# Key lookup: every second tile's eight rows of values fetched by indirect DMA and summed on VectorE

## The chip, the cores and the metric

The kernel runs on one core of one Trainium2 chip. The time is that of the device from start to end, in microseconds, the median of three runs. The engines are TensorE (PE in the rows, its weight loads PEld), VectorE (DVE), ScalarE (ACT), GpSimd (POOL) and SyncE (SP), which issues the transfers. Lines such as L2246 are lines of the kernel before; the changed kernel has 47 lines more, so the same function stands some 30 to 50 lines lower in it.

## The reference

A two-layer model: a Mamba block, a mixture-of-experts attention, a rotary attention, and last a lookup of keys, the only part that the change touches. T is 4096 tokens of width 256. Cut to what matters:

```
x3     = x2 + context @ Wo.T + bo                  # end of the attention layer
xh     = layernorm(x3)
query  = xh @ q_proj.T                             # 128 wide
scores = (query @ R.T) @ (keys @ R.T).T / sqrt(48) + reliability   # 1024 keys
top, idx = top_k(scores, 8)
look   = sum_k softmax(top)_k * values[idx_k]      # values: 1024 rows of 256
learned = unc_w2 . gelu(xh @ unc_w1.T + b1)        # one number a token
gate   = sigmoid(f(sigmoid(learned), log(1 + var(xh)) / its mean))
out    = x3 + xh + gate * look
```

## The kernel before

The lookup is the function key_lookup, the last of the program. It takes the 4096 tokens in 8 chunks of 512 tokens, each of 4 tiles of 128 tokens (a token lies on a partition). Every engine has its own program, written out by hand in one fixed order, and the engines wait for each other by semaphores alone. Chunks 0 to 5 run in loops on the hardware; chunks 6 and 7 are written out.

Per chunk: flip_ctx and x3_pair (twice, two tiles each) make x3 in the PSUM bank pX, and add puts it into SBUF on VectorE. normalize is the layernorm: four statistics, seven small operations, one power on GpSimd (L2188), four normalizing operations (L92). flip_xh, move_xh, project, route and move_rq make the router's query of the chunk; widen, hidden and learn make the learned number. keep stores x3 + xh and its statistics.

Per tile: scores multiplies 128 tokens by 1024 keys into one of two PSUM buffers (pS). pick takes the eight largest on VectorE (MAX8, L2231) and writes a copy in which these eight are replaced by a mark (MATCH_REPLACE8, L2233). expo takes the exponential of all 1024 scores on ScalarE. weigh (L2239) multiplies it by "is marked", which leaves eight weights among 1024 zeros, and sums them. flip_weights turns the 128 x 1024 weights over on TensorE, move_weights copies them to SBUF, lookup multiplies them by all 1024 rows of values (L2510, 16 passes through the array), and finish (L2246) scales the result by one over the sum.

The body of VectorE's loop shows in which order this goes for one chunk:

```
weigh(n + 1, 1); pick(n + 2, 0, base); finish(n, 0)
weigh(n + 2, 0); pick(n + 3, 1, base + TILE_MARKS); finish(n + 1, 1)
keep(c + 1, base)
weigh(n + 3, 1); pick(n + 4, 0, base); add(c + 2, 0); finish(n + 2, 0)
add(c + 2, 1); normalize(c + 2, base)
weigh(n + 4, 0); pick(n + 5, 1, base); finish(n + 3, 1); learned(c + 1)
```

GpSimd does two things a chunk: the bias (L2186) on the loaded x2, and the power of the layernorm. At the end results (L2272) makes the output, four operations a chunk, once the gate is known.

Of the kernel before, what the change touches and what calls it, by code (L numbers as in the profile page):

```python
# [12 lines left out]
ALU = mybir.AluOpType  # L13
ACT = mybir.ActivationFunctionType
AXIS_X = mybir.AxisListType.X
ds = bass.ds
# [5 lines left out]
NT = T // TILE  # L22
# [2098 lines left out]
def key_lookup(nc, a, p):  # L2121
# [3 lines left out]
    GONE = -3.0e38  # L2125
    with Scope(nc, "look") as s:
# [8 lines left out]
        top, ntop = s.sb("top", [128, 2, TOP]), s.sb("ntop", [128, 2])  # L2135
        left, expd, weight = s.sb("left", [128, 2, NK]), s.sb("expd", [128, 2, NK]), s.sb("weight", [128, 2, NK])
# [21 lines left out]
        out_ready, winv_ready = s.sem("out_ready"), s.sem("winv_ready")  # L2158
        one_set = s.sem("one_set")
# [5 lines left out]
        with nc.Block() as block:  # L2165
# [13 lines left out]
            def _(pool):  # L2179
# [4 lines left out]
                with pool.Fori(0, NCH) as c:  # L2184
                    pool.wait_ge(c_in, (c + 1) * 32)
                    nc.gpsimd.tensor_tensor(x2[:], x2[:], b_o[:].unsqueeze(1).broadcast_to([128, TPC, D]), ALU.add).then_inc(biased, 1)  # L2186
                    pool.wait_ge(var_ready, c + 1)
                    nc.gpsimd.tensor_tensor(rstd[:], var[:], mhalf[:], ALU.pow).then_inc(rstd_ready, 1)  # L2188

            KEEP_MARKS = TPC + 2  # L2190
# [3 lines left out]
            def _(dve):  # L2194
# [30 lines left out]
                def pick(n, b, base):  # L2225

                    ch = Chain(dve, dve_sem, base)
                    at_least(dve, weight_ready, n - 1)
                    dve.wait_ge(s_psum, n + 1)
                    ch.mark(nc.vector.memset(wsum[:, b:b + 1], 0.0))  # L2230
                    ch.step(nc.vector.max(top[:, b, :], pS[:, b, :]))  # L2231
                    nc.vector.tensor_scalar(ntop[:, b:b + 1], top[:, b, 0:1], -1.0, None, ALU.mult).then_inc(ntop_ready, 1)
                    nc.vector.match_replace(out=left[:, b, :], in_to_replace=top[:, b, :], in_values=pS[:, b, :], imm_value=GONE).then_inc(left_ready, 1)  # L2233
                    assert ch.n == TILE_MARKS

                def weigh(n, b):
                    dve.wait_ge(exp_ready, n + 1)
                    at_least(dve, wt_psum, n - 1)
                    nc.vector.scalar_tensor_tensor(weight[:, b, :], left[:, b, :], GONE, expd[:, b, :], ALU.is_equal, ALU.mult, accum_out=wsum[:, b:b + 1]).then_inc(weight_ready, 1)  # L2239
                    dve.wait_ge(weight_ready, n + 1)  # L2240
                    nc.vector.reciprocal(winv[:, ds(n, 1)], wsum[:, b:b + 1]).then_inc(winv_ready, 1)

                def finish(n, b):
                    dve.wait_ge(winv_ready, n + 1)
                    dve.wait_ge(look_psum, n + 1)
                    nc.vector.tensor_scalar(look_all[:, ds(n, 1), :], pL[:, 0:D], winv[:, ds(n, 1)], None, ALU.mult).then_inc(look_ready, 1)  # L2246
# [433 lines left out]
```

## Time and profile before

| | |
|---|---|
| median of 3 runs | 3569.22 us (3567.5 to 3570.5) |
| the profiled execution | 3561.59 us, its span 3559.8 us |
| key lookup in the span | from 3213.8 us to 3555.35 us |
| busy in the whole span | TensorE 91%, VectorE 77%, ScalarE 63%, GpSimd 27% |

The profiled execution is one of many, 7.6 us below the median of the runs. Differences of about 0.2% (7 us) are what a measurement of this kernel can tell from none. The lookup is some 340 us of it; shares over the whole span say little about it.

### The profile page before, as it was taken

How to read it: one execution, taken by the hardware profiler on the slowest of the kernel's cores; microseconds unless marked ns; L12 is line 12 of the kernel's file. 1: busy time of each engine (PE TensorE's matmuls, PEld its weight loads, DVE VectorE, ACT ScalarE, POOL GpSimd, SP SyncE). 2: the span in 40 equal slices, each digit the busy share in tenths (PEclk: the TensorE clock that was granted, in tenths of full speed). 3: DMA queues.
4: the chain of work that ended last, by engine and by line, in shares of the span. 5: the costliest groups of instructions: out<-in, count | busy, mean ns of one | idle time of the engine just before them, and what ended most of it. 6: DMA issues, size and time to landing. Idle time of an engine off the chain costs nothing. (4 is left out here: it accounts for less than half of the span.)

```text
span 3559.8 us, 54793 instructions
## 1 busy us (share of the span) xinstructions
PE 3222.1 (91%) x17996; PEld 1622.3 (46%) x18162; DVE 2750.6 (77%) x4129; ACT 2234.5 (63%) x3972; POOL 965.3 (27%) x907
## 2 busy tenths in 40 slices
PE   7868888988899998998799999999999999997897
PEld 3327777777566666775322222222222222224665
DVE  6739999999466664456888888888888888854666
ACT  5669999999100002222278888888788888883343
POOL 7639999998000000003200000000000000001100
PEclk9979999999899999999889999999999999998999
DMA  4656443420311416422400000000000000001001
GB/s 136 197 176 149 119 109 96 105 62 13 113 57 35 104 32 155 118 60 75 124 8 14 21 14 22 15 21 15 22 15 21 15 21 14 26 4 33 29 24 48
DMA packets 219079, 216.75 MB, mean 61 GB/s; under 512 B 63986, under 2 KB 165490, under 8 KB 218036
## 3 DMA queue, kind: packets, MB, share of 16 engines
q1 hardware_dynamic: 218820, 213.41, 21.9%
q8 instruction: 149, 2.44, 0.3%
q14 instruction: 110, 0.90, 0.1%
HBM read 145.99 MB, written 67.37 MB: 60 GB/s over the span
## 5 line engine op out<-in xcount | busy, mean ns | idle before, releaser
L1975 DVE TENSOR_REDUCE attn_part_max<-attn_pM 128x1 f32<-128x1024 f32 x1024 | 1204.4, 1219 | 162.8 <-PE attn_pM L2029 159.3
L1955 ACT ACTIVATE attn_probs<-attn_pE 128x512 f32<-128x512 f32 x2048 | 1089.8, 597 | 205.7 <-PE attn_pE L2078 196.4
L2078 PE MATMUL attn_pE<-attn_q,attn_k_exp 128*128 128x512 bf16 x1882 | 590.5, 385 | 54.6 <-ACT attn_q L1927 24.7
L2049 PE MATMUL attn_pA<-attn_probs,attn_v 128*32 128x512 f32 x4096 | 560.7, 604 | 2.0 <-issue 1.0
L648 DVE TENSOR_TENSOR_SCAN scan_h<-scan_abar,scan_states,scan_dbu 128x512 f32<-128x512 f32 x384 | 458.3, 1252 | 0.0
L2078 PEld LDWEIGHTS attn_pE<-attn_q,attn_k_exp 128*128 128x128 bf16 x2048 | 139.1, 97 | 609.0 <-ACT attn_probs L1955 462.4
L662 PE MATMUL scan_hT<-scan_ident,scan_h 128*128 128x128 f32 x2048 | 322.5, 281 | 71.3 <-ACT scan_hcT L600 29.0
L1908 POOL TENSOR_TENSOR attn_peak_parts<-attn_peak,attn_zero 128x4 bf16<-128x4 f32 x128 | 26.4, 206 | 1278.2 <-DVE attn_peak L1979 1278.2
L600 ACT ACTIVATE scan_hcT<-scan_hT,scan_c_t 128x512 f32<-128x512 f32 x512 | 366.4, 716 | 1.1 <-PE scan_hT L662 1.1
L2028 PE MATMUL attn_pM<-attn_k_exp,attn_q 64*128 64x512 bf16 x1024 | 326.1, 392 | 23.3 <-DVE attn_part_max L1975 15.1
L1173 PE MATMUL moe_pP<-moe_w_qkv,moe_xT 128*128 128x384 f32 x1024 | 340.3, 490 | 0.9
L2029 PE MATMUL attn_pM<-attn_k_max,attn_q 64*128 64x512 bf16 x1024 | 326.1, 392 | 0.0
L672 PE MATMUL scan_y_acc<-scan_ident,scan_hcT 128*128 128x128 f32 x2048 | 304.2, 274 | 1.2 <-DVE scan_g_even L631 0.6
L662 PEld LDWEIGHTS scan_hT<-scan_ident,scan_h 128*128 128x128 f32 x2048 | 224.2, 142 | 167.9 <-DVE scan_h L648 112.4
L589 POOL TENSOR_TENSOR scan_dbu<-scan_du_odd,scan_b_odd 128x2048 f32<-128x2048 f32 x64 | 289.7, 4557 | 8.9 <-DVE scan_h L648 8.9
L589 POOL TENSOR_TENSOR scan_dbu<-scan_du_even,scan_b_even 128x2048 f32<-128x2048 f32 x64 | 289.2, 4553 | 7.3 <-DVE scan_h L648 5.2
L1173 PEld LDWEIGHTS moe_pP<-moe_w_qkv,moe_xT 128*128 128x128 f32 x1024 | 193.5, 191 | 131.7 <-DVE moe_acc L1043 4.3
L672 PEld LDWEIGHTS scan_y_acc<-scan_ident,scan_hcT 128*128 128x128 f32 x2048 | 240.6, 143 | 4.6 <-issue 2.5
L1046 DVE SCALAR_TENSOR_TENSOR moe_acc<-moe_pP,moe_rw,moe_acc 128x192 f32<-128x192 f32 x448 | 161.9, 411 | 76.2 <-PE moe_pP L1173 75.5
L2028 PEld LDWEIGHTS attn_pM<-attn_k_exp,attn_q 64*128 64x128 bf16 x1024 | 83.1, 93 | 293.8 <-issue 158.5
L613 ACT ACTIVATE scan_abar<-scan_delta_even,scan_decay 128x512 f32<-128x512 f32 x256 | 188.9, 738 | 7.9 <-DVE scan_h L648 7.9
L613 ACT ACTIVATE scan_abar<-scan_delta_odd,scan_decay 128x512 f32<-128x512 f32 x256 | 182.7, 714 | 8.5 <-DVE scan_h L648 8.5
(282 smaller groups left out, 3874.4 us busy)
## 6 DMA issues: line engine op xcount, KB each, us to landing
scan_b_even<-mid_BC SPq DMA_DIRECT2D x16, 1024.0 KB, 10.2
scan_b_odd<-mid_BC SPq DMA_DIRECT2D x16, 1024.0 KB, 9.6
causal_rwB<-mid_rwT SPq DMA_DIRECT2D x64, 256.0 KB, 4.5
attn_q<-mid_q_parts SPq DMA_DIRECT2D x224, 64.0 KB, 2.4
mid_gT<-front_gT SPq DMA_DIRECT2D x8, 1024.0 KB, 8.4
mid_uT<-front_uT SPq DMA_DIRECT2D x8, 1024.0 KB, 9.7
mid_dT<-scan_g_odd SPq DMA_DIRECT2D x8, 1024.0 KB, 4.3
moe_yT<-mid_yT SPq DMA_DIRECT2D x7, 1024.0 KB, 6.7
```

The lines of the kernel that those rows point to most:

```text
L589: nc.gpsimd.tensor_tensor(dbu[:, G % NDBU, :, :], du[u % 2][:], b_row, ALU.mult).then_inc(dbu_ready, 1)
L600: nc.scalar.activation(hcT[:, i % NHC, :], hT[:, i % 2, :], ACT.Copy, scale=c_t[:, u * TPC + tile, n:n + 1]).then_inc(hc_ready, 1)
L613: nc.scalar.activation(abar[:, k % 2, :], delta[u % 2][:, m, :], ACT.Exp, scale=decay[:, m, n:n + 1]).then_inc(abar_ready, 1)
L648: nc.vector.tensor_tensor_scan(h[:, G % NH, m, :], abar[:, k % 2, :], dbu[:, G % NDBU, m, :], state, ALU.mult, ALU.add).then_inc(scan_done, 1)
L662: last = nc.tensor.transpose(hT[:, i % 2, m * 128:(m + 1) * 128], h[:, G % NH, m, tile * 128:(tile + 1) * 128], ident[:])
L672: last = nc.tensor.matmul(y_acc[:, m, tile * 128:(tile + 1) * 128], hcT[:, i % NHC, m * 128:(m + 1) * 128], ident[:], start=(n == 0 and ti ...
L1173: last = nc.tensor.matmul(pP[:, n % NP, 0:2 * QKV], xT[:, c % 2, k, j * 128:(j + 1) * 128], w_qkv[:, k, pr * 2 * QKV:(pr + 1) * 2 * QKV], ...
L1955: nc.scalar.activation(probs[:, kt % 4, h, :], pE[:, bank(item), :], ACT.Exp, scale=SCALE).then_inc(exp_done, 1)
L1975: nc.vector.reduce_max(part_max[:, h, j, i:i + 1], pM[:, m % 2, :], AXIS_X).then_inc(max_read, 1)
L2028: nc.tensor.matmul(pM[:, m % 2, 0:CH], q[0:64, qc, h, j * 128:(j + 1) * 128], k_exp[0:64, par, i * CH:(i + 1) * CH], start=True, stop=True)
L2049: last = nc.tensor.matmul(pA[32 * h:32 * h + 32, :], v[:, par, kt, :], probs[:, kt % 4, h, :], start=(kt == 0), stop=(kt == KT - 1))
L2078: nc.tensor.matmul(pE[:, bank(item), :], k_exp[:, par, kt * 128:(kt + 1) * 128], q[:, qc, h, :], start=True, stop=True).then_inc(e_psum, 1)
```

## The change

Of the four tiles of a chunk, tiles 0 and 2 ("even") are done as before. Tiles 1 and 3 ("odd") are no longer weighed, flipped, moved and multiplied. Instead place_top takes the eight largest scores and their places (MAX_INDEX), expo_top takes the exponential of the eight alone, gather issues eight indirect DMAs from GpSimd (each fetches one row of values for each of the 128 tokens, 128 KB), and add_rows sums the eight rows by their weights on VectorE. add_rows of a tile stands one odd tile later in the order than its place_top. pS keeps two buffers: one for even tiles, one for odd ones. GpSimd's loop is written out. The core of the diff:

```diff
+                def gather(o):
+
+                    pool.wait_ge(place_ready, o + 1)
+                    pool.wait_ge(sum_ready, AHEAD + o - 1)
+                    for k in range(TOP):
+                        nc.gpsimd.indirect_dma_start(rows[:, o % 2, k, :], None, a["values"], bass.IndirectOffsetOnAxis(place[:, o % 2, k:k + 1], 0)).then_inc(rows_in[o % 2], 16)
+
+                for c in range(2):
+                    bias(c)
+                    root(c)
+                gather(0)
+                for c in range(NCH):
+                    if c + 2 < NCH:
+                        bias(c + 2)
+                    gather(2 * c + 1)
+                    if c + 2 < NCH:
+                        root(c + 2)
+                    if c + 1 < NCH:
+                        gather(2 * c + 2)
...
+                def place_top(c, j):
+
+                    o, b = 2 * c + j // 2, j // 2 % 2
+                    dve.wait_ge(s_psum, c * TPC + j + 1)
+                    nc.vector.memset(gate8[:], 0.0).then_inc(cleared, 1)
+                    nc.vector.max(top8[:, b, :], pS[:, 1, :]).then_inc(top8_ready, 1)
+                    dve.wait_ge(top8_ready, o + 1)
+                    nc.vector.tensor_scalar(ntop8[:, b:b + 1], top8[:, b, 0:1], -1.0, None, ALU.mult).then_inc(ntop8_ready, 1)
+                    nc.vector.max_index(place[:, b, :], top8[:, b, :], pS[:, 1, :]).then_inc(place_ready, 1)
...
+                def add_rows(c, j):
+
+                    o, b = 2 * c + j // 2, j // 2 % 2
+                    dst = look_all[:, ds(c * TPC + j, 1), :]
+                    dve.wait_ge(exp8_ready, o + 1)
+                    nc.vector.reciprocal(inv8[:, b:b + 1], sum8[:, b:b + 1]).then_inc(sum_step, 1)
+                    dve.wait_ge(sum_step, o * SUM_STEPS + 1)
+                    nc.vector.tensor_scalar(w8[:, b, :], e8[:, b, :], inv8[:, b:b + 1], None, ALU.mult).then_inc(sum_step, 1)
+                    dve.wait_ge(sum_step, o * SUM_STEPS + 2)
+                    dve.wait_ge(rows_in[b], (c + 1) * 16 * TOP)
+                    nc.vector.tensor_scalar(dst, rows[:, b, 0:1, :], w8[:, b, 0:1], None, ALU.mult).then_inc(sum_step, 1)
+                    for k in range(1, TOP):
+                        dve.wait_ge(sum_step, o * SUM_STEPS + 2 + k)
+                        nc.vector.scalar_tensor_tensor(dst, rows[:, b, k:k + 1, :], w8[:, b, k:k + 1], dst, ALU.mult, ALU.add).then_inc(sum_step if k < TOP - 1 else sum_ready, 1)
...
+                    pick(c, 2, base)
+                    finish(c, 0)
+                    weigh(c, 2)
+                    place_top(c, 3)
+                    base = base + TILE_MARKS
+                    keep(c + 1, base)
+                    base = base + KEEP_MARKS
+                    pick(c, 4, base)
+                    base = base + TILE_MARKS
+                    add_rows(c, 1)
                     if ahead == 2:
                         add(c + 2, 0)
-                    finish(n + 2, 0)
+                    finish(c, 2)
                     if ahead == 2:
                         add(c + 2, 1)
                         normalize(c + 2, base)
                         base = base + CHUNK_LN_MARKS
...
+                    weigh(c, 4)
+                    place_top(c, 5)
+                    add_rows(c, 3)
+                    learned(c + 1)
```

In the last chunk add_rows(7, 1) stands ahead of the first results and add_rows(7, 3) ahead of the last four.

The first place is TensorE, from the middle of the loop's chunk: before, the query's product (L2479, project) is followed by a tile's flip of weights (look_pT<-look_ident,look_weight), its scores (look_pS) and later its lookup (look_pL).

```order
L2448 MATMUL look_pT<-look_ident,look_xh 128x128 x8
L2510 MATMUL look_pL<-look_values,look_weightT 128x256 x8
L2479 MATMUL look_pX<-look_xT,look_w_q 128x512 x2
L2460 REGISTER_ALU
L2448 MATMUL look_pT<-look_ident,look_weight 128x128 x8
L2503 MATMUL look_pS<-look_rk,look_rq 128x512 x2
L2484 MATMUL look_pX<-look_query,look_w_r 128x512
L2452 ISA
L2448 MATMUL look_pT<-look_ident,look_ctx 128x128 x8
L2510 MATMUL look_pL<-look_values,look_weightT 128x256 x8
L2489 MATMUL look_pX<-look_xT,look_w_u 64x512 x2
```

The same place on TensorE after the change, where L2529 is project, L2558 scores and L2566 lookup.

```order
L2497 MATMUL look_pT<-look_ident,look_xh 128x128 x8
L2566 MATMUL look_pL<-look_values,look_weightT 128x256 x8
L2526 REGISTER_ALU
L101 REGISTER_ALU
L2529 MATMUL look_pX<-look_xT,look_w_q 128x512 x2
L2558 MATMUL look_pS<-look_rk,look_rq 128x512 x2
L2534 MATMUL look_pX<-look_query,look_w_r 128x512
L2501 ISA
L2497 MATMUL look_pT<-look_ident,look_ctx 128x128 x8
L2539 MATMUL look_pX<-look_xT,look_w_u 64x512 x2
```

The flip and the lookup of tile 1 are gone; the scores of tile 3 still stand behind project, which waits for the copy of xh.

The second place is VectorE, in the loop behind keep: before, a tile's weigh is followed by the next pick and the first add.

```order
L2239 SCALAR_TENSOR_TENSOR look_weight,look_wsum<-look_left,look_expd 128x1024
L2241 ISA
L2241 RECIPROCAL look_winv<-look_wsum 128x1
L2229 REGISTER_ALU
L2230 MEMSET look_wsum 128x1
L2231 MAX look_top<-look_pS 128x8
L44 REGISTER_ALU
L2232 TENSOR_SCALAR look_ntop<-look_top 128x1
L2233 MATCH_REPLACE look_left<-look_top,look_pS 128x1024
```

After the change VectorE has there the pick of an even tile and then add_rows; the last two rows come seven times in all.

```order
L2265 MAX look_top<-look_pS 128x8
L44 REGISTER_ALU
L2266 TENSOR_SCALAR look_ntop<-look_top 128x1
L2267 MATCH_REPLACE look_left<-look_top,look_pS 128x1024
L2299 RECIPROCAL look_inv<-look_sum 128x1
L2300 ISA
L2301 TENSOR_SCALAR look_w<-look_e,look_inv 128x8
L2302 REGISTER_ALU
L2303 ISA
L2304 ISA
L2304 TENSOR_SCALAR look_look_all<-look_rows,look_w 128x256
L2306 REGISTER_ALU
```

Ten operations in a row, each of which waits for the one before it, now stand between the pick and the first add.

The third place is GpSimd after the change: the start and two chunks (L2196 bias, L2200 the power of the layernorm, L2207 the gathers).

```order
L2196 TENSOR_TENSOR look_x<-look_x,look_b_o 128x1024
L2200 TENSOR_TENSOR look_rstd<-look_var,look_mhalf 128x4
L2207 DMA look_rows<-in_values,look_place 128x256 x8
L2196 TENSOR_TENSOR look_x<-look_x,look_b_o 128x1024
L2207 DMA look_rows<-in_values,look_place 128x256 x8
L2200 TENSOR_TENSOR look_rstd<-look_var,look_mhalf 128x4
```

The power, for which VectorE's layernorm waits, now stands behind sixteen gathers a chunk; before, only the bias stood ahead of it.

## Rows read from the trace of the kernel before

**Rows 1.** The chain that ended last, in order of time: start us, us, what

```profile
3331.28 1.03 POOL look_rstd L2188
...
3359.56 1.92 PE look_pX L2471 x8
...
3421.32 1.09 ACT look_xT L2358 x2
...
3422.63 1.98 PE look_pX L2479 x4
...
3484.14 1.03 POOL look_rstd L2188
```

**Rows 2.** Busy time by window: two chunks, then the last stretch; last columns clock, DMA share, GB/s

```profile
3367.62:3443.93 76.31, 68.40 (x326) 48.87 (x328) 50.65 (x125) 30.35 (x42) 7.66 (x4) 0.98 0.08 27
3484.14:3555.35 71.21, 58.03 (x265) 42.42 (x263) 51.50 (x122) 27.85 (x38) 1.02 (x1) 0.93 0.15 52
```

**Rows 3.** Waits of four chunks: engine line waited for, us in total, times, longest

```profile
DVE look_look_all L2246 <- PE look_pL L2510: 26.0, 12, 3.4
```

**Rows 4.** Groups by line, lookup stage: count, then busy us, mean ns, then idle

```profile
L2510 PE MATMUL look_pL<-look_values,look_weightT 128*128 128x256 f32 x512 | 126.2, 403 | 8.6 <-ACT look_weightT L2358 4.5 <-DVE look_look_all L2246 4.1
...
L2272 DVE SCALAR_TENSOR_TENSOR look_result<-look_look_all,look_gate,look_sum_all 128x256 f32<-128x256 f32 x32 | 12.9, 474 | 1.9 <-ACT look_gate L2440 1.8
```

**Rows 5.** Timeline of VectorE, one chunk: start us, us, engine, line, operation

```profile
3366.70 0.76 DVE L2200 TENSOR_TENSOR look_x<-look_pX,look_x 128x256 f32<-128x256 f32 x2 [1.05 <-PE look_pX L2471]
...
3370.93 1.38 DVE L92 TENSOR_SCALAR look_xh<-look_x,look_st,look_rstd 128x256 f32<-128x256 f32 x4 [1.13 <-POOL look_rstd L2188]
3372.53 1.22 DVE L2239 SCALAR_TENSOR_TENSOR look_weight<-look_left,look_expd 128x1024 f32<-128x1024 f32 x1 [0.23 <-DVE look_xh L92]
...
3373.91 0.16 DVE L2241 RECIPROCAL look_winv<-look_wsum 128x1 f32 x1
...
3374.05 1.23 DVE L2231 MAX8 look_top<-look_pS 128x8 f32<-128x1024 f32 x1
3375.32 0.15 DVE L2232 TENSOR_SCALAR look_ntop<-look_top 128x1 f32<-128x1 f32 x1
...
3376.59 0.47 DVE L2246 TENSOR_SCALAR look_look_all<-look_pL,look_winv 128x256 f32 x1
...
3377.91 1.22 DVE L2239 SCALAR_TENSOR_TENSOR look_weight<-look_left,look_expd 128x1024 f32<-128x1024 f32 x1 [0.77 <-ACT look_expd L2390]
...
3394.42 1.22 DVE L2214 TENSOR_TENSOR look_sum_all<-look_x,look_xh 128x1024 f32 x1
...
3397.41 1.23 DVE L2239 SCALAR_TENSOR_TENSOR look_weight<-look_left,look_expd 128x1024 f32<-128x1024 f32 x1
```

**Rows 6.** Timeline of all engines, single rows of it

```profile
3230.09 2.35 POOL L2186 TENSOR_TENSOR look_x<-look_x,look_b_o 128x1024 f32<-128x1024 f32 x1 [2.33 <-DMA look_x<-mid_x]
...
3230.76 2.75 DVE L2214 TENSOR_TENSOR look_sum_all<-look_x,look_xh 128x1024 f32<-128x1024 f32 x1
...
3231.61 3.56 PE L2479 MATMUL look_pX<-look_xT,look_w_q 128*128 128x512 f32 x4 [1.22 <-DVE look_rk L2282]
...
3367.62 0.37 SPq L1757 DMA_DIRECT2D look_ctx<-mid_ctx  x1
...
3387.28 1.13 PE L2503 MATMUL look_pS<-look_rk,look_rq 49*128 49x512 f32 x4
```

**Rows 7.** Busy time by window, around a pause of TensorE

```profile
3375.98:3378.90 2.92, 0.00 (x0) 0.00 (x0) 2.15 (x4) 2.09 (x3) 0.00 (x0) 0.88 0.00 0
3378.90:3381.00 2.10, 2.10 (x9) 2.10 (x10) 1.92 (x8) 0.00 (x0) 0.00 (x0) 0.50 0.00 0
```

**Rows 8.** DMA issues: names, count, KB each, median us to landing

```profile
mid_ctx<-attn_ctx SPq DMA_DIRECT2D x32, 128.0 KB, 2.0
```

**Rows 9.** Timeline of the last chunk

```profile
3523.86 0.19 DVE L2255 SCALAR_TENSOR_TENSOR look_var_v<-look_tmp_v,look_var_v 128x32 f32<-128x32 f32 x1
...
3529.84 1.11 ACT L2390 ACTIVATE look_expd<-look_pS,look_ntop 128x1024 f32<-128x1024 f32 x1
```

More of the change, by code:

```diff
@@ L2125, in key_lookup @@
     GONE = -3.0e38
+    AHEAD = 2
     with Scope(nc, "look") as s:
@@ L2158, in key_lookup @@
         out_ready, winv_ready = s.sem("out_ready"), s.sem("winv_ready")
+        top8_ready, ntop8_ready, place_ready, exp8_ready, sum_step, sum_ready, cleared = (s.sem(n) for n in (
+            "top8_ready", "ntop8_ready", "place_ready", "exp8_ready", "sum_step", "sum_ready", "cleared"))
+        rows_in = [s.sem(f"rows_in_{i}") for i in range(2)]
         one_set = s.sem("one_set")
@@ L2318, in body @@
                         base = base + CHUNK_LN_MARKS
-                    if ahead:
-                        weigh(n + 4, 0)
-                        pick(n + 5, 1, base)
-                        base = base + TILE_MARKS
-                    finish(n + 3, 1)
-                    if ahead:
-                        learned(c + 1)
+                    weigh(c, 4)
+                    place_top(c, 5)
+                    add_rows(c, 3)
+                    learned(c + 1)
                     return base
@@ L2332, in _ @@
                 variances(ch)
-                n, first = NT - TPC, ch.n
-                weigh(n + 1, 1)
-                pick(n + 2, 0, marks + ch.n)
-                finish(n, 0)
+                last = NCH - 1
+                pick(last, 2, marks + ch.n)
                 ch.n += TILE_MARKS
-                weigh(n + 2, 0)
-                pick(n + 3, 1, marks + ch.n)
-                ch.n += TILE_MARKS
+                finish(last, 0)
+                weigh(last, 2)
+                place_top(last, 3)
                 gate_input(ch)
-                finish(n + 1, 1)
-                weigh(n + 3, 1)
+                add_rows(last, 1)
                 dve.wait_ge(gate_ready, 1)
@@ L2346, in _ @@
                     results(c)
-                finish(n + 2, 0)
+                finish(last, 2)
                 for c in range(NCH // 2, NCH - 1):
                     results(c)
-                finish(n + 3, 1)
-                results(NCH - 1)
+                add_rows(last, 3)
+                results(last)
             @block.scalar
@@ L2428, in _ @@
                 body(NCH - 2, 1, 1)
-                n = NT - TPC
-                move_weights(n)
+                last = NCH - 1
+                move_weights(2 * last)
                 act.wait_ge(var_all, 1)
```

185 lines of the change are left out of this document (88 added, 97 removed).

## The prediction

> **What bounds the kernel now.** I read the chain that ended last first. In the steady part of the lookup it repeats chunk by chunk, and the power of the layernorm marks one place of it: from 3331.28 to 3484.14 us four chunks pass, 38.2 us each [rows 1]. The windows then say who works in such a chunk: TensorE is busy 68.4 of 76.3 us, VectorE 50.7, ScalarE 30.4, GpSimd 7.7 [rows 2]. The waits say who waits for whom: VectorE's longest is for lookup's product, 26.0 us in four chunks, 6.5 a chunk [rows 3]. So TensorE sets the pace now, and VectorE is the next: 25.3 us of work a chunk, with waits between that are mostly for TensorE.
>
> **What goes.** An odd tile loses its lookup on TensorE (126.2 us over 32 tiles, 3.9 a tile [rows 4]) and its flip, eight transposes, about a microsecond. That is some 10 us a chunk off TensorE: 34.2 becomes 24. ScalarE loses the big exponential and two copies an odd tile. If TensorE alone counted, a chunk would fall by almost all its waits too. It doesn't, because of what VectorE gets.
>
> **What comes on VectorE, step by step round one chunk.** I walk the new loop body from the start of pick(c,2), with durations from [rows 5]:
> - pick to weigh, with the exponential between: 3374.05 to 3377.91, 3.86 us; weigh and the reciprocal until the next MAX8: 3372.53 to 3374.05, 1.52. That makes 5.4.
> - place_top(c,3) can't start there: its scores stand on TensorE behind project, and project behind move_xh, which on ScalarE stands behind the exponential. Exponential done at about 3.8; copy to project 1.31, project 1.98 [rows 1]; scores 1.13 [rows 6]: 8.2. A new wait of 2.8 us, where the odd tile's weigh and finish used to lie.
> - place_top: MAX_INDEX isn't in the trace. The nearest is MATCH_REPLACE8, which also reads 1024 scores behind a load of eight values, so place_top is taken as pick, 2.54 (3374.05 to 3376.59): 10.7. keep, 2.99: 13.7. pick(c,4): 16.3.
> - add_rows(c,1): two small operations of 0.15 and a gap of 0.04 between dependent ones (MAX8 ends 3375.28, the next starts 3375.32), 0.4; then eight of 256 elements in a chain. A scalar_tensor_tensor of this shape lasts 474 ns [rows 4], with the gap 0.51, so 4.0. Together 4.4: 20.7.
> - The first add, half of the x3 pairs, 0.79: 21.5. x3_pair's second half waits for it, as before, and takes 1.92 [rows 1] with nothing left to do on VectorE but one finish: 23.5.
> - Second add, statistics, power, until L92: 3366.70 to 3370.93, 4.23: 27.7. L92 to weigh 1.60, weigh 1.52: 30.9. place_top 2.54, add_rows 4.4, learned 0.15: **38.0 us** round.
>
> So VectorE's own round, 32 us of work and 6 of waits, is as long as TensorE's was: 38.0 against 38.2. What TensorE gives up, VectorE takes.
>
> **Two additions with bounds.** First, the waits in add_rows have counts from registers in the loops. The gap in front of the reciprocal behind weigh, also with such a count and an address from a register, is up to 0.16 (3373.75 to 3373.91) against 0.04. Some 20 such steps a chunk: 0 to 2.4 us. I take 1.0, since the plain register waits in the trace are nearer to the small gap. Second, TensorE's clock. After the last weigh (30.9) come flip, the copy behind expo_top, flip_xh and lookup, so TensorE is done at about 38.8, and the next project comes at 38.0 + 5.1: a pause of some 4.3 us. In the trace a pause of 2.92 us ended with the granted clock at 0.50, the lower level of 1.2 GHz, for the work behind it [rows 7]. project lasted 3.56 us at that level against 1.98 [rows 6, 1], and scores 1.1 more: up to 2.7 us, and both lie in VectorE's wait. The other pauses of the round have slack behind them. 0 to 2.7; I take the middle, 1.4, since such falls came behind some pauses and not behind others.
>
> A chunk then takes 40.4 us, 2.2 more than now, in the six loop chunks: 13.2.
>
> **The last stretch.** From the last power to the end it is 71.2 us now [rows 2]. On VectorE after it: L92 and weigh 4.2, place_top 2.5, add_rows and learned 4.5; chunk 6 without adds and layernorm 8.2 + 2.5 + 3.0 + 2.5 + 4.4 + 0.4 + 1.5 + 2.5 + 4.5 = 29.5; variances and the exponential behind three table loads, 7.1 from 3523.86 to 3530.95 [rows 9], of which a copy takes some, 6.6; weigh, place_top, the gate's small operations 5.1; add_rows 4.3; 32 result operations of 0.40 [rows 4], 12.9; a finish 0.4; add_rows 4.3. That is 74.3, 3.1 more; with the clock's 1.4 in chunk 6, 4.5. The start is left as it is: the same kinds of step in the same places.
>
> **The gathers.** No GpSimd DMA is in the trace. From below: SP issues one in 0.37 us [rows 6]. From above: a 128 KB transfer lands in 2.0 us [rows 8]; if GpSimd handled one at a time it would be 2.4 a gather. I take 1.4, the middle. GpSimd's round is: power to L92 1.1, L92 1.6, weigh 1.5, place_top 2.5, eight gathers, bias 2.4 [rows 6], eight gathers, 9.1 + 16g. At 1.4 that is 31.5 us, and VectorE's round hides it; add_rows stands one odd tile behind its place_top, so 8 x 1.4 + 2 us of landing are hidden too. The cover is gone at g = 1.96: from there each 0.1 us a gather costs 1.6 us a chunk, because the power stands behind the gathers. At 0.37 it makes no difference; at 2.4 the round is 47.5.
>
> The Trainium skill (DMA: Bandwidth & Descriptors, section Anatomy of one DMA) puts a DMA from GpSimd at about 2.0 us plus its bytes over 436 GB/s, most of it completion rather than issue; as an estimate that is 2.3 us for 128 KB. By that time as the step from one gather to the next the round would be 46 us and the kernel some 3635; by its words most of this overlaps, as in the sum. No row of GpSimd issuing shows which.
>
> **Sum.** 13.2 + 4.5 = +17.7: 3561.6 becomes 3579.3 in the profiled execution, which lies 7.6 under the median; 3569.2 becomes **3587**. With both additions at nothing: -0.2 x 6 + 3.1 = +2, 3571. With both full: 4.9 x 6 + 3.1 + 2.7 = +35, 3604.
>
> **Rivals.**
> - *The gathers bind* (0.22). For: 16 a chunk in order with the layernorm's power on one engine that can't be passed. Against: GpSimd has 30 us idle a chunk. Time at 2.4: 9.3 x 6 = 56, 9 in chunk 6, about 8 in the last, 3 of the sum: 3645. A second way there: VectorE and GpSimd hold each other up. The row of keep lasted 2.75 us beside the bias, against 1.22 alone [rows 6, 5]. If the gathers hold up add_rows and weigh as the bias held up keep, by 1.5 us for a pair, four stretches a chunk make +6: 3623.
>   The Trainium skill (SBUF — State Buffer, section Who interferes with whom) says that a VectorE instruction with two SBUF inputs contends with a GpSimd one that reads SBUF, and add_rows has seven such a tile. The pair of rows on keep agrees; that a gather reads long enough to matter no run here shows.
> - *No change* (0.14). Neither addition comes: a round of 38.0, 3571 and around. Against: the pause before project is longer than the one that lowered the clock.
> - *Faster* (0.09). Unrelated operations of this shape follow each other every 0.40 us [rows 4]. If the dependent ones of add_rows did too, each add_rows would be 0.8 shorter, a round 36.4 with both additions at nothing, and the kernel -1.8 x 6 + 3.1 - 3.2, -11: 3558. It decides for faster by more than 0.2% once the round is under 36.5. Against: the gap behind a dependent operation in the rows.
> - *The forecast* (0.55): VectorE's round of 38.5 to 43 us, 3576 to 3604.
>
> **Numbers.** About 0.2% (7 us) is what can be told from no change. Faster 0.09, same 0.14, slower 0.77. The range leaves out the faster case below 3568 and the gathers at over 2.4 us: 3568 to 3645.
>
> **What would show it.** In the changed profile, the window of two steady chunks should have VectorE at 31 to 33 us a chunk and TensorE at 24 to 28; the power's rows should stand 39 to 42 us apart; VectorE's largest wait should be MAX8 for scores, 2.5 to 5.5 a chunk, and none for look_pL; add_rows 4.2 to 5.5 us from its reciprocal to its last sum; project near 3.5 us in some chunks. GpSimd's power should start within 0.3 us of look_var, and L92 wait 1.1; if L92 waits longer, the gathers bind. A gather over 1.96 us, an add_rows with waits for its rows, or a place_top much off 2.5 would make the forecast wrong.

## The result, and the profile after

The changed kernel takes 3578.45 us (median of 14 runs) against 3568.99 for the kernel before (14 runs on the same chip): a ratio of 1.0029, 95% interval 1.0020 to 1.0037, 9.5 us slower where the forecast had 17.7. Its profiled execution took 3577.77 us, with a span of 3575.7; that is 16.2 more than the profiled execution of before, which lay 7.4 under its own median, while this one lies 0.7 under.

The layernorm's power marks the chunks again. First the timeline of GpSimd after the change (start us, us, engine, line, operation; in brackets the idle time before it and what ended it):

```profile
3252.42 1.02 POOL L2200 TENSOR_TENSOR look_rstd<-look_var,look_mhalf 128x4 f32<-128x4 f32 x1 [18.38 <-DVE look_var L89]
...
3373.71 1.03 POOL L2200 TENSOR_TENSOR look_rstd<-look_var,look_mhalf 128x4 f32<-128x4 f32 x1 [6.12 <-DVE look_var L89]
...
3380.90 1.02 POOL L2207 DMA_INDIRECT look_rows<-in_values,look_place  x1 [6.15 <-DVE look_place L2278]
3382.23 1.09 POOL L2207 DMA_INDIRECT look_rows<-in_values,look_place  x1 [0.30 <-issue]
3383.62 0.95 POOL L2207 DMA_INDIRECT look_rows<-in_values,look_place  x1 [0.30 <-issue]
...
3391.28 2.36 POOL L2196 TENSOR_TENSOR look_x<-look_x,look_b_o 128x1024 f32<-128x1024 f32 x1
...
3495.43 1.03 POOL L2200 TENSOR_TENSOR look_rstd<-look_var,look_mhalf 128x4 f32<-128x4 f32 x1 [5.62 <-DVE look_var L89]
```

From 3252.42 to 3495.43 lie six chunks: 40.5 us each. In the kernel before the same six took 233.05 us, 38.8 each, of which [rows 1] showed the last four. Most gathers occupy GpSimd for 0.94 to 1.1 us (median 0.96), the first of a group of eight for up to 1.9, and the next starts 0.30 later. In the loop's chunks GpSimd has waited 5.6 to 7.4 us for VectorE's variances in front of the power; VectorE then waits 1.15 us, for the power itself.

The windows of two chunks and of the last stretch. The columns, as in [rows 2], are the length, the busy time of TensorE, its weight loads, VectorE, ScalarE and GpSimd, the granted clock, the DMA share and GB/s:

```profile
3373.71:3454.82 81.11, 60.02 (x230) 38.22 (x229) 59.89 (x148) 22.80 (x38) 40.56 (x37) 0.82 0.26 78
3495.43:3571.15 75.72, 41.77 (x148) 26.26 (x148) 63.81 (x155) 20.72 (x34) 33.48 (x33) 0.73 0.34 104
```

TensorE fell from 34.2 to 30.0 us a chunk, less than the lookup that left, because its granted clock is now 0.82 where it was 0.98: much of what remains runs at the lower level. VectorE went from 25.3 to 29.9 and GpSimd from 3.8 to 20.3. Both busy times miss what the prediction wanted to see here, 31 to 33 us for VectorE and 24 to 28 for TensorE. The last stretch takes 75.7 us where it took 71.2.

The waits of 3340 to 3500, four chunks (what waited, for what; us in total, times, longest), in place of [rows 3]:

```profile
POOL look_rstd L2200 <- DVE look_var L89: 24.4, 4, 7.0
DVE look_top L2275 <- issue: 15.4, 4, 4.4
DVE look_x L2233 <- PE look_pX L2521: 8.7, 4, 3.1
DVE look_xh L92 <- POOL look_rstd L2200: 4.6, 4, 1.2
...
DVE look_look_all L2292 <- PE look_pL L2566: 0.8, 1, 0.8
```

The wait for lookup's product, 26.0 us before, is 0.8. In its place stand MAX8's wait for the odd tile's scores, 3.9 us a chunk, and the second add's for x3's second half, 2.2. Both can be seen in the timeline, first of VectorE in one chunk, then of TensorE:

```profile
3381.48 3.63 DVE L2307 SCALAR_TENSOR_TENSOR look_look_all<-look_rows,look_w,look_look_all 128x256 f32 x7
...
3393.31 1.23 DVE L2275 MAX8 look_top<-look_pS 128x8 f32<-128x1024 f32 x1 [2.55 <-issue]
...
3394.71 1.23 DVE L2278 FIND_INDEX8 look_place<-look_top,look_pS 128x8 uint32<-128x1024 f32 x1
3395.85 1.21 DVE L2247 TENSOR_TENSOR look_sum_all<-look_x,look_xh 128x1024 f32 x1
...
3410.86 0.76 DVE L2233 TENSOR_TENSOR look_x<-look_pX,look_x 128x256 f32<-128x256 f32 x2 [3.10 <-PE look_pX L2521]
```

```profile
3383.43 5.10 PE L2566 MATMUL look_pL<-look_values,look_weightT 128*128 128x256 f32 x16
3390.21 1.98 PE L2529 MATMUL look_pX<-look_xT,look_w_q 128*128 128x512 f32 x4 [1.68 <-issue]
...
3407.42 3.40 PE L2521 MATMUL look_pX<-look_w_o,look_ctxT 128*128 128x256 f32 x8 [2.86 <-DVE look_x L2233]
...
3430.72 3.67 PE L2529 MATMUL look_pX<-look_xT,look_w_q 128*128 128x512 f32 x4 [3.23 <-ACT look_xT L2410]
```

The seven dependent sums take 3.63 us, 0.52 each. FIND_INDEX8, the search for the eight places, is as long as MATCH_REPLACE8 (1.22 us). TensorE's clock is at its lower level behind this pause of 2.86 us (x3's second half takes 3.40 instead of 1.92). At the projection it is at either level: in the five chunks from 3300 to 3500 us the projection takes 1.98, 3.45, 1.98, 3.67 and 3.40.

### The profile page after: what moved, and what is told of

The parts are those of the page before. It is cut to its first block and busy times, and to the rows that moved or that the text cites. A ratio compares the mean times of both kernels' runs of the same rounds, so it can differ in the third digit from the quotient of the medians.

```text
span 3575.7 us, 54417 instructions
## 1 busy us (share of the span) xinstructions
PE 3206.9 (90%) x17778; PEld 1574.1 (44%) x17778; DVE 2788.6 (78%) x4225; ACT 2204.7 (62%) x3956; POOL 1097.8 (31%) x1035
## 5 line engine op out<-in xcount | busy, mean ns | idle before, releaser
L2078 PE MATMUL attn_pE<-attn_q,attn_k_exp 128*128 128x512 bf16 x2048 | 628.7, 385 | 31.3 <-ACT attn_q L1927 24.7
## 6 DMA issues: line engine op xcount, KB each, us to landing
scan_b_even<-mid_BC SPq DMA_DIRECT2D x16, 1024.0 KB, 10.7
```

The costliest lines, as they stand in the source:

```text
L2078: nc.tensor.matmul(pE[:, bank(item), :], k_exp[:, par, kt * 128:(kt + 1) * 128], q[:, qc, h, :], start=True, stop=True).then_inc(e_psum, 1)
```

## The experiments

A table of all runs first. The ratio is to the kernel before on the same chip, and "us a chunk" the mean distance of the power's rows over the last five chunks that have one, in the profiled execution.

| kernel | median us | ratio (95%) | us a chunk |
|---|---|---|---|
| before | 3568.99 | 1 | 38.5 |
| before, profiled again | 3566.97 (one run) | | 39.0 |
| changed | 3578.45 | 1.0029 (1.0020, 1.0037) | 40.7 |
| no gathers | 3580.45 | 1.0036 (1.0026, 1.0047) | 40.8 |
| gathers twice | 3700.72 | 1.0367 (1.0344, 1.0390) | 53.5 |
| scores first | 3576.93 | 1.0025 (1.0014, 1.0035) | 40.1 |
| four rows summed | 3550.26 | 0.9954 (0.9937, 0.9970) | 35.8 |
| add first | 3569.03 | 1.0008 (0.9998, 1.0018) | 38.7 |
| 36 idle matmuls | 3579.11 | 1.0039 (1.0025, 1.0053) | 40.1 |
| scores and place_top first | 3576.07 | 1.0032 (1.0020, 1.0045) | 39.7 |
| three orders, 22 idle matmuls | 3576.52 | 1.0028 (1.0017, 1.0039) | 38.1 |
| 19 idle matmuls | 3579.65 | 1.0035 (1.0023, 1.0046) | 40.5 |
| three orders, bias moved | 3560.89 | 0.9981 (0.9972, 0.9990) | 37.5 |
| the same, 11 idle matmuls | 3563.24 | 0.9990 (0.9981, 0.9998) | 37.6 |

The last two columns can't be turned into each other directly, since the executions also differ ahead of the chunks. In seven of the fourteen traces, those of the kernel before and of the changed one among them, the second power stands 24.2 to 24.4 us behind the first; in the other seven (gathers twice, scores first, four rows, add first, 36 and 19 idle matmuls, three orders with 22) 27.4 to 27.7. The program is the same there; the difference is TensorE's clock in the matmuls that begin the lookup. The widening (granted clock 1.00 in the changed kernel, 0.50 in add first), in this order:

```profile
3239.26 1.90 PE L2539 MATMUL look_pX<-look_xT,look_w_u 128*64 128x512 f32 x4 [0.93 <-ACT look_rq L2431]
```

```profile
3243.96 3.65 PE L2539 MATMUL look_pX<-look_xT,look_w_u 128*64 128x512 f32 x4 [0.93 <-ACT look_rq L2431]
```

**No gathers.** The indirect DMAs go; SyncE fills both row buffers once.

```diff
-                    for k in range(TOP):
-                        nc.gpsimd.indirect_dma_start(rows[:, o % 2, k, :], ...).then_inc(rows_in[o % 2], 16)
...
+                    sp.dma_start(rows[:, i, :, :], a["values"].rearrange("(k p) n -> p k n", p=128)).then_inc(rows_in[i], 16)
```

> The 128 indirect DMAs are left out; both row buffers are filled once with rows of the values table by SyncE's queue, so the odd tiles sum wrong rows with their right weights, by the same VectorE instructions. Theory, VectorE's round sets the pace and the gathers are hidden: the same time as the changed kernel, 3578 us within 4, power rows still 40.7 us apart. Rival, GpSimd's queue holds up the layernorm's power or its descriptor work holds up VectorE's two-operand instructions: each chunk shorter by 1 us or more, so 3572 or less; if the whole difference to the kernel before came from them, 3569.

The time did not fall: 3580.45, an interval that overlaps the changed kernel's. Its waits in the same four chunks:

```profile
POOL look_rstd L2202 <- DVE look_var L89: 139.3, 4, 35.5
...
DVE look_top L2274 <- issue: 17.1, 4, 4.4
```

GpSimd idles 35 us a chunk in front of the power and nothing starts earlier; MAX8 waits 4.3 us a chunk, for 3.9 with the gathers. All 112 sums take 54.3 us here and 54.7 with the gathers. So the gathers, as they are, cost VectorE neither waits nor speed. The first rival of the prediction falls, in both of its ways.

**Gathers twice.** Each gather is issued a second time, into a spare buffer.

```diff
                         nc.gpsimd.indirect_dma_start(rows[:, o % 2, k, :], ...).then_inc(rows_in[o % 2], 16)
+                        nc.gpsimd.indirect_dma_start(again[:, o % 2, k, :], ...).then_inc(rows_in[o % 2], 16)
```

> Each gather is issued twice, the second time into a spare buffer that nobody reads, and the sums wait for all sixteen of a tile. By the changed kernel's trace a gather lasts 0.96 us and the next starts 0.30 later, 1.26 in all, so GpSimd's round becomes 9.1 + 32 x 1.26 = 49.4 us against VectorE's 40.7. Theory, the cover of the gathers is gone once GpSimd's round is longer than VectorE's: 8.7 us more a chunk, some 52 in six chunks and 5 to 15 at the end, 3635 to 3650 us, and L92 waiting for the power. Rival, a gather's cost is mostly completion that overlaps, and issue could go faster once more stand in the queue: under 3600. Rival, gathers in flight also slow VectorE: its add_rows instructions of 0.518 us pitch become longer and the time goes over 3650.

3700.72: the cover has an end, and the cost behind it is larger than expected, 53.5 us a chunk instead of 49.4, and 118.5 us from the last power to the end where I allowed 5 to 15 more than 80. Part of this is plain: behind the last power stand four tiles of sixteen gathers, 81 us, which I had not counted. And GpSimd's step was 1.33 us on average, with the long first gathers, where I had put 1.26: that makes 2 of the 4 us a chunk. The other part the trace does not explain:

```profile
3466.68 0.95 POOL L2209 DMA_INDIRECT look_again<-in_values,look_place  x1 [0.30 <-issue]
3470.65 0.48 DVE L2294 TENSOR_SCALAR look_look_all<-look_pL,look_winv 128x256 f32 x1 [10.68 <-DMA attn_k_exp<-mid_k_parts]
3474.22 1.04 POOL L2201 TENSOR_TENSOR look_rstd<-look_var,look_mhalf 128x4 f32<-128x4 f32 x1 [6.59 <-DVE look_var L89]
```

This finish needs lookup's product, and that was done at 3459.3. VectorE stood still for 10.7 us, until 3 us after the last gather, and the releaser that is named, a DMA of an earlier stage, can't be it. The power then waited for VectorE. ScalarE has such gaps of 2 to 7 us ahead of the same copy in each chunk. They were absent in the changed kernel's steady part; what they wait for stays open. The DMA view of 3459 to 3471 has packets of GpSimd's queue alone, so no fetch of instructions is seen in the gap. The last of my rivals there, slower sums, is answered: the 112 sums take 54.7 us, as in the changed kernel, although the time went over 3650. The median of a gather did not change with twice as many in the queue (0.95 for 0.96).

**Scores first.** On TensorE the odd tile's scores stand ahead of lookup and project.

```diff
+                    scores(c, 3, cpar)
                     lookup(c, 0)
...
                         project(c + 1, (c + 2) * TPC)
                         pe.wait_ge(xh_moved, c + 2)
-                    scores(c, 3, cpar)
```

> The scores of the second odd tile of a chunk stand on TensorE ahead of the even tile's lookup and the next chunk's projection. Theory, MAX8's wait for them (3.9 us a chunk in the changed kernel's trace) is part of VectorE's binding round: 2.6 to 3.9 us less a chunk, 16 to 23 in six chunks, so 3555 to 3563 us; MAX8 in place_top waits under 1.5 us a chunk. Rival, the round is held by TensorE's own work and clock or by GpSimd: the wait only moves to another instruction, 3574 to 3580 us.

A miss: 0.6 us a chunk, not 2.6. The timeline says where it went:

```profile
3384.34 1.97 PE L2497 MATMUL look_pT<-look_ident,look_xh 128*128 128x128 f32 x8
3386.23 2.08 PE L2558 MATMUL look_pS<-look_rk,look_rq 49*128 49x512 f32 x4
3388.24 5.49 PE L2566 MATMUL look_pL<-look_values,look_weightT 128*128 128x256 f32 x16
...
3393.99 0.48 DVE L2292 TENSOR_SCALAR look_look_all<-look_pL,look_winv 128x256 f32 x1 [3.35 <-PE look_pL L2566]
3394.39 2.69 DVE L2284 SCALAR_TENSOR_TENSOR look_weight<-look_left,look_expd 128x1024 f32<-128x1024 f32 x1
```

MAX8 in place_top no longer waits. But the finish of the even tile, which is ahead of weigh on VectorE, waits 3.35 us in this chunk for a lookup that starts 2 us later and takes 5.49 us where another takes 3.62. Over five chunks this is the smaller part; the waits of 3300 to 3500:

```profile
DVE look_top L2265 <- issue: 13.8, 5, 5.5
...
DVE look_look_all L2292 <- PE look_pL L2566: 5.5, 4, 3.3
```

L2265 is the MAX8 of pick. In the changed kernel the two had waited 0.4 and 1.5 us there, and place_top's MAX8 17.9: of these 17.9, 13.4 came back at the next chunk's first scores, which still stand behind project, and 4.0 at the finish. Weigh's 2.69 us instead of 1.23 is in this chunk alone of the five; it began 0.8 us behind GpSimd's bias, of which more below. VectorE, which works in order, met TensorE at the next instructions that need it.

**Four rows summed.** Only four of the eight rows are summed; all are fetched.

```diff
+            SUMMED = 4
...
-                    for k in range(1, TOP):
+                    for k in range(1, SUMMED):
```

> Only four of the eight gathered rows are summed for each odd tile; all eight are still fetched. That is four scalar_tensor_tensor of 0.518 us less for each of 16 tiles. Theory, VectorE's round binds and the sums lie on it: 4.1 us less a chunk, 33 us in all, 3545 us. Behind half of the sums a pause of TensorE gets shorter as well, so a few us more may go. Rival, the sums fill time in which VectorE would wait anyway for TensorE or for the rows: under 10 us less, 3568 to 3578, and a new wait of VectorE takes their place.

The powers of the last five chunks, first and last:

```profile
3295.28 1.04 POOL L2200 TENSOR_TENSOR look_rstd<-look_var,look_mhalf 128x4 f32<-128x4 f32 x1 [4.56 <-DVE look_var L89]
...
3474.23 1.03 POOL L2200 TENSOR_TENSOR look_rstd<-look_var,look_mhalf 128x4 f32<-128x4 f32 x1 [4.47 <-DVE look_var L89]
```

35.8 us a chunk, 4.9 less, and 27 us by the ratios against 33 expected. The 4.1 us taken from VectorE's sums come off the chunk in full, with 0.8 us more that was waiting. VectorE's round sets the pace.

**Add first.** The first add of the chunk after next is put ahead of the odd tile's sums.

```diff
-                    add_rows(c, 1)
                     if ahead == 2:
                         add(c + 2, 0)
+                    add_rows(c, 1)
                     finish(c, 2)
```

> On VectorE the first add of the chunk after next stands ahead of the sums of the odd tile, so that TensorE's second half of the x3 pairs runs beside them. In the changed kernel TensorE pauses 2.86 us ahead of that half, which then takes 3.40 us at half clock or 1.99 at full, and the second add waits 2 to 3.1 us for it, 8.7 us in four chunks. Theory, this wait lies on VectorE's binding round: 2.2 us less a chunk, 13 in six, 3565 us, and no wait above 0.5 us before the second add. Rival, as in the run with the scores first the wait only moves along (to L92's power, or to MAX8 and the finish, because TensorE pauses longer elsewhere and its clock falls there): within 4 us of 3578.

2.0 us less a chunk, as the wait's 2.2 said. The waits of 3300 to 3500, of MAX8 and of the adds, where the wait for x3's second half had been 12.2 (the releaser named is a transfer of an earlier stage and can't be it):

```profile
DVE look_top L2275 <- issue: 17.3, 5, 5.1
...
DVE look_x L2233 <- DMA rot_w_qk<-in_w_qk: 3.3, 5, 0.7
```

MAX8 waits as before (17.3 for 17.9), so this one wait didn't move on. The kernel is 7.5 us faster than the changed one by the ratios, where 13 were expected, and can't be told from the kernel before. In its trace the six chunks are 13.0 us shorter, and the second power comes 6.5 us later: 3.4 of that lie ahead of the first power, and 3.1 are the slower start told above.

**Idle matmuls, 36 and 19.** They fill three pauses of TensorE.

```diff
+                        fill(16, pT[:, 0, 0:D])    # 8 in the second kernel, behind learn
...
+                        fill(10, pT[:, 0, 0:D])    # 5, ahead of x3_pair(c + 2, 1)
...
+                        fill(10, pX[:, 0:D])       # 6, ahead of project(c + 1, ...)
```

> The changed kernel with 36 idle matmuls a chunk on TensorE (256 columns each, into accumulator banks that are free at that time, read by nobody): 16 after the learned values, 10 ahead of the second half of the x3 pairs, 10 ahead of the projection, each group shorter than the pause that it fills if it runs at full clock. Theory, TensorE's half clock behind its pauses costs VectorE's round 1 to 3 us a chunk (project 1.7 us longer in every other chunk, x3's second half 1.4, flips, scores and lookup some 5 in front of project): granted clock 1.0 in the lookup, 2.6 us less a chunk, 16 in all, about 3562 us. Rival, the low clock is harmless since what it lengthens has slack: 3575 to 3581. Rival, the idle matmuls get in the way and the clock stays low: slower than 3581.

> The changed kernel with 19 idle matmuls a chunk (8, 5 and 6 in the same three pauses) where the run before had 36: there each was recorded as two of 0.225 us, so a group of 16 took 7.2 us instead of 3.6, TensorE was busy 199 of 200 us and set the pace itself, 40.1 us a chunk. Theory, with groups that fit the pauses the clock stays at 1.0, MAX8's wait falls from 3.9 to 2.8 us a chunk and x3's second half takes 1.99: 2 to 2.6 us less a chunk than the changed kernel, 12 to 16 in six, 3562 to 3567 us. Rival, the low clock has slack behind it: 3574 to 3581.

Neither gained. 3300 to 3500 us of the first, then of the second, with the columns of the windows:

```profile
3300.00:3500.00 200.00, 199.27 (x929) 148.06 (x928) 149.15 (x370) 57.17 (x95) 101.55 (x90) 1.00 0.25 74
```

```profile
3300.00:3500.00 200.00, 174.26 (x756) 117.07 (x757) 147.22 (x367) 56.94 (x95) 101.34 (x90) 0.96 0.25 74
```

With 36, each of which is recorded as two, the clock was 1.00 throughout, and MAX8's wait fell to 12.8 us in five chunks, 2.6 each: this is near the 2.8 that the walk gave without the clock's addition. But TensorE was busy 199.27 of 200 us, and the chunk stayed at 40.1; that it bound by itself there is my reading. With 19 there was time again, and the pause ahead of the projection stayed (2.05 us, project 2.98): MAX8 waited 19.2 us in five. The clock's price on that wait is then about 1.3 us a chunk (3.9 less 2.6), as an estimate; a kernel that gains it was not found.

**Scores and place_top first.** Scores as above; on VectorE place_top before weigh, the finish behind it.

```diff
                     pick(c, 2, base)
+                    place_top(c, 3)
+                    weigh(c, 2)
                     finish(c, 0)
-                    weigh(c, 2)
-                    place_top(c, 3)
```

> The scores of the odd tile stand first on TensorE, as in the run before (which gained 1.3 us where 16 to 23 were expected, since the finish of the even tile, ahead of weigh on VectorE, then waited 3.35 us for the later lookup). Here VectorE's order is changed too: place_top of the odd tile right behind pick, then weigh, then the finish. Theory, both waits go: in the run before they were 3.35 for the finish and some 0.8 for the exponential a chunk, so 3.5 to 4 us less a chunk than the changed kernel, 3554 to 3558 us. Rival, TensorE's longer way behind its pauses (flips, scores and lookup at half clock) is what VectorE waits for, wherever the wait stands: 3572 to 3578.

A miss again, 3576.07: the waits of place_top and of the finish went, and something else came. VectorE and GpSimd in one chunk:

```profile
3387.39 3.96 DVE L2284 SCALAR_TENSOR_TENSOR look_weight<-look_left,look_expd 128x1024 f32<-128x1024 f32 x1
```

```profile
3387.91 2.35 POOL L2196 TENSOR_TENSOR look_x<-look_x,look_b_o 128x1024 f32<-128x1024 f32 x1
```

Weigh reads two SBUF tiles and takes 1.23 us alone. Beside the bias it takes 3.96, 2.7 more, and ends 1.1 us behind the bias, which keeps its 2.35. It is so in all five chunks (3.93 to 4.01), always with weigh recorded as starting some 0.5 us ahead of the bias. It is the pair of [rows 6] (keep at 2.75 beside the bias) in a new place. In the changed kernel the bias fell at 3391.28, where VectorE waited for MAX8's scores anyway; with that wait gone they met in every chunk. With the gathers no such thing shows (the sums' 54.7 and 54.3 us above).

**Three orders, 22 idle matmuls.** The add first as well, 16 idle matmuls behind learn, 6 ahead of project.

> All together: scores of the odd tile first on TensorE, place_top ahead of weigh and the finish behind it, the first add ahead of the sums, and 22 idle matmuls a chunk in the two pauses that are left (16 after the learned values, 6 ahead of the projection). Theory, VectorE's round keeps little beside its 31 us of work, the power's 1.15 and one short wait: 33.5 to 35 us a chunk against 40.7, so 34 to 43 us less in six chunks, 3536 to 3545 us, below the kernel before. Rival, GpSimd's round becomes the longer one (9.1 + 16 x 1.26 = 29.3 us, so only if its gathers are late): L92 waits over 2 us and the time stays above 3550.

3576.52, far from the 3536 to 3545. Weigh took 3.95 beside the bias, and the 16 idle matmuls, 7.17 us, held up the flip behind them. After the loop VectorE waited 10.2 us for scores; on the way to it ScalarE's copy of the query started 3.3 us after the projection was done, a gap without a releaser like those above.

**Three orders, bias moved.** No idle matmuls; the bias starts only after weigh, in GpSimd's wait for the places.

```diff
+                bias(2, 1)                         # the second number: waits for that count of weight_ready
                 gather(0)
                 for c in range(NCH):
-                    if c + 2 < NCH:
-                        bias(c + 2)
                     gather(2 * c + 1)
                     if c + 2 < NCH:
                         root(c + 2)
+                    if c + 3 < NCH:
+                        bias(c + 3, 2 * c + 3)
                     if c + 1 < NCH:
                         gather(2 * c + 2)
```

> No idle matmuls. Scores of the odd tile first on TensorE, place_top ahead of weigh and the finish behind it, the first add ahead of the sums; and GpSimd's bias is moved to where it waits anyway, between the layernorm's power and the next gathers, and starts only after weigh. In the run with these orders and 22 idle matmuls the bias (2.35 us) had come to lie beside weigh, which then took 3.95 us instead of 1.23. Theory, this collision and TensorE's clock are what kept the reordered kernels at 38 us a chunk: without the collision 2.7 us less, MAX8 waiting about 2 to 3 us for scores at half clock, 36.5 to 37.5 a chunk, 3555 to 3562 us. Rival, GpSimd's operation slows whatever VectorE does beside it, scores too: the MAX8 and FIND_INDEX8 that now lie beside the bias get longer, and nothing is gained, 3566 to 3574.

3560.89: 0.9981, 7 us faster than the kernel before by an interval that leaves out 1, and 17 us faster than the changed one. No run moves the bias alone: against scores and place_top first (39.7 us a chunk for 37.5) the place of the first add changed as well. In its timeline weigh is short, and MAX8 and FIND_INDEX8, which read PSUM, aren't touched by the bias beside them:

```profile
3381.46 1.21 DVE L2287 SCALAR_TENSOR_TENSOR look_weight<-look_left,look_expd 128x1024 f32<-128x1024 f32 x1
3390.85 1.23 DVE L2268 MAX8 look_top<-look_pS 128x8 f32<-128x1024 f32 x1 [4.51 <-issue]
...
3406.51 1.23 DVE L2278 MAX8 look_top<-look_pS 128x8 f32<-128x1024 f32 x1
3407.92 1.23 DVE L2281 FIND_INDEX8 look_place<-look_top,look_pS 128x8 uint32<-128x1024 f32 x1
```

```profile
3406.32 2.35 POOL L2198 TENSOR_TENSOR look_x<-look_x,look_b_o 128x1024 f32<-128x1024 f32 x1 [3.05 <-DVE look_weight L2287]
```

One large wait is left, 4.5 us a chunk: the next chunk's first scores, behind project, route, widen and a flip on TensorE.

**The same with 11 idle matmuls.**

> The same as the run just above, with 11 idle matmuls a chunk (8 after the learned values, 3 ahead of the projection), half of what was there before. Theory, VectorE's round is its 31 us of work, the power's wait of 1.15 and under 2 us of others: 33.5 to 35.5 us a chunk, 3543 to 3555 us, faster than the kernel before. Rival, the clock doesn't matter once the orders are changed: the same as the run without idle matmuls, within 4 us. Rival, they delay the flip that follows: slower than it by 5 or more.

3563.24, within 4 us of the run without them: the first rival's time. The clock rose from 0.77 to 0.93 over 3300 to 3500, but not in front of the first scores. In one chunk:

```profile
3379.80 1.46 PE L2596 MATMUL look_pX<-look_w_o,look_ident 128*128 128x256 f32 x6
3383.51 3.62 PE L2532 MATMUL look_pX<-look_xT,look_w_q 128*128 128x512 f32 x4 [2.25 <-ACT look_xT L2413]
```

The three idle matmuls ahead of the projection ended 2.25 us too early, the projection took 3.62 us instead of 1.98, and MAX8 waited 5.30 us behind it.

**Before, profiled again.**

> The kernel before, profiled once more: its first profiled execution lay 7.4 us under the median of its times. Theory, such executions differ ahead of the lookup or in its first chunks and not in its steady part: power rows again 38.2 us apart. Rival, the steady part itself differs from one execution to the next, by 1 us a chunk or more.

```profile
3293.46 1.02 POOL L2188 TENSOR_TENSOR look_rstd<-look_var,look_mhalf 128x4 f32<-128x4 f32 x1 [34.78 <-DVE look_var L89]
...
3488.23 1.02 POOL L2188 TENSOR_TENSOR look_rstd<-look_var,look_mhalf 128x4 f32<-128x4 f32 x1 [32.45 <-DVE look_var L89]
```

39.0 us a chunk instead of 38.5, its mean clock 0.967 against 0.970: the rival in kind, if not in size. One chunk, from the power at 3410.10 to that at 3449.69, took 39.6 us where the first execution took 38.1. The steady part does differ between executions, by up to 1.5 us in a chunk. Of the 5.4 us between the two executions 2.0 lie ahead of the second power, 2.1 in the six chunks and 1.3 behind the last power.

## Why the prediction was right, point by point

- **The mechanism held, at about half of the size.** The wait for TensorE's lookup went, VectorE's own round took its place, with MAX8 waiting for the scores behind the projection. Leaving out eight sums a chunk took off their full time, and taking away the gathers took off nothing. But of the 17.7 us forecast 9.5 were measured; the last point says where the rest went.
- **The round, 38.0, with 1.0 and 1.4 added, 40.4: measured 40.5.** place_top 2.54 and 2.54 measured, with the search read off a different operation. add_rows 4.4, measured 4.5 and 4.8. The waits with a count from a register, 1.0: the gaps behind learned, ahead of the two tiles' first sums and ahead of pick's next MAX8 are 0.18, 0.15, 0.28 and 0.54, 1.2 together. The work in the walk counts the small gaps between dependent operations, which is why it says 32 us where VectorE was busy for 29.9. (The 68.4 of 76.3 us that the prediction gives TensorE "in such a chunk" are those of two chunks; its sums take them so.)
- **The clock's 1.4 had about the right size, and a part of it the wrong place.** It was the middle of two bounds. I put it at the projection and the scores behind a pause of 4.3 us. The pause there was 1.7 to 3.5, and another of 3.77 lay ahead of the flip; the projection ran at the lower level in three chunks of five (MAX8's wait 3.9 for 2.8, 1.1 more). The rest, some 0.7, fell on x3's second half, which took 1.99 to 3.78 in the six chunks (mean 2.70), where the prediction had said "The other pauses of the round have slack behind them." That one had none.
- **The last stretch, +4.5: 71.2 became 75.7.** Its pieces: 11.4 us until chunk 6 (11.2 forecast), 31.2 for chunk 6 (30.9 with the clock's 1.4), 5.9 for the variances and the exponential (6.6), 4.9 for the next step (5.1). To the tenth it is luck.
- **The gathers, 1.4 with bounds 0.37 and 2.4: 1.26 for most, 1.35 on average.** The middle of so wide bounds lay this near by luck; what mattered was to be under 1.96, and with 5.6 us or more to spare ahead of the power the cover held. The Trainium skill (DMA: Bandwidth & Descriptors, section Anatomy of one DMA) puts most of its fixed 2.0 us down to completion and not to setup. The trace agrees as far as it goes: the step on GpSimd is 1.26 us for most gathers, under those 2.0, and as many gathers again left it there.
- **The contention.** VectorE's weigh, with two SBUF inputs, is held up by the bias (3.96 us for 1.23), and the sums, which have two as well, are not by a gather: 54.7 us with them, 54.3 without. The Trainium skill (SBUF — State Buffer, section Who interferes with whom) names this pair, two SBUF inputs on VectorE beside a GpSimd instruction that reads SBUF, and the trace agrees. It also says that the one that issues first keeps the shared ports and the other blocks. The trace does not bear that out by the recorded starts: weigh starts at 3387.39 and the bias at 3387.91, and weigh is the one that is lengthened.
- **What failed is a size: the base.** "A chunk then takes 40.4 us, 2.2 more than now, in the six loop chunks: 13.2." The 40.4 was right and the "now" was not. The 38.2 of now is the mean of the last four chunks; all six took 38.8 in that execution, and 39.2 in the one profiled again. So the six gave 10.0 us against the first profile (7.9 against the second). (Their first power stands at 3251.09 and 3253.09, at 3252.42 in the changed kernel.) And the profiled execution, "which lies 7.6 under the median", lent its offset to the forecast as if it belonged to the kernel; the changed kernel's lies 0.7 under. Of the 8.5 us between 3587 and 3578.45, 6.9 are this offset, and 1.5 the sum: 3.2 less in the chunks, 1.3 more ahead of them and 0.4 more elsewhere.

The expectations of the experiments erred more than the prediction. Three times a wait on VectorE's round was taken as its price (scores first, scores and place_top first, all orders with idle matmuls), and each time the next meeting with TensorE or GpSimd took the room. The kernels with idle matmuls missed their times as well. The one wait that was worth its length a chunk stood in front of the second add, and there the other waits stayed as they were.

## What to carry to other kernels

Where the second engine of a pair stands only a quarter behind in busy time (25.3 us against 34.2 here), work moved onto it can buy nothing: walk its whole round with the new work in it, waits included, before counting what the first engine saves. By these runs a wait in front of one instruction is worth its length only if nothing later on that engine needs the same producer and nothing on another engine had been hiding in it; the bias that cost nothing beside a waiting VectorE cost 2.7 us a chunk once VectorE stopped waiting. And count a difference against the same rows, over the same chunks, of more than one execution of the kernel before.

## What the runs showed of the hardware that was not expected

- An indirect DMA of 128 rows of 1 KB occupies GpSimd for 0.96 us (the median; the first of a group 1.0 to 1.9), plus 0.30 to the next. With 16 in a row instead of 8 the median is 0.95 and the gap again 0.30.
- A VectorE scalar_tensor_tensor of 1024 elements with two SBUF inputs that starts 0.5 us ahead of a GpSimd tensor_tensor of the same size ends 1.1 us after it: 3.96 us instead of 1.23, while GpSimd keeps its 2.35. One that starts 0.8 us behind it (scores first) ends 1.1 us after it too: 2.69. MAX8 and FIND_INDEX8 on PSUM beside the same operation stay at 1.23.
- TensorE's clock at the start of the lookup is at either of its levels in the same program text (widening 1.90 us at a granted clock of 1.00, or 3.65 at 0.50), which moves everything behind it by 3.1 us.
- With the gathers doubled, VectorE and ScalarE stood still 2 to 11 us with everything done that the program waits for there. The changed kernel has no such gap in its steady part. The cause was not settled.
